# The first tile of x and the first chunk of weights in one transfer, in a 16-batch mixture-of-experts kernel

## The reference

```python
g = einsum('bsd,edf->ebsf', h, Wg)           # E=8, D=128, F=512
u = einsum('bsd,edf->ebsf', h, Wu)
expert_outs = einsum('ebsf,efd->ebsd', silu(g) * u, Wd)
expert_output = einsum('be,ebsd->bsd', gating_probs, expert_outs)
shared = einsum('bsf,fd->bsd', silu(h @ Sg) * (h @ Su), Sd)
x = x + (1.0 - sg) * expert_output + sg * shared
...
x = x + einsum('bij,bjk->bik', T[itok - 1], x)
```

## Time and profile before

| | |
|---|---|
| median of 3 runs | 307.83 us (307.63 to 792.65) |
| the profiled execution's own time | 307.79 us |
| its span in the profile | 306.0 us |
| PE busy / weight loads | 302.3 us (99%) / 250.9 us (82%) |
| DVE, ACT, POOL busy | 214.5, 162.8, 102.2 us |
| instructions | 4476 |

### The profile page before, as it was taken

The page is one execution under the profiler, slowest core; times in us unless marked ns, Lnnn a source line. Parts: engine busy times, 40 slices in busy tenths (PEclk is TensorE's granted clock), DMA queues, the critical chain, the costliest instruction groups (busy, mean ns, idle before and its releaser), DMA issues.

```text
span 306.0 us, 4476 instructions
## 1 busy us (share of the span) xinstructions
PE 302.3 (99%) x1348; PEld 250.9 (82%) x1348; DVE 214.5 (70%) x350; ACT 162.8 (53%) x302; POOL 102.2 (33%) x116
## 2 busy tenths in 40 slices
PE   8999999999999999999999999999999999999996
PEld 8888888888888888888888888888888888888885
DVE  3677667766776676667766776677667666787974
ACT  5755555555555555555555555555555555554562
POOL 3675114431244115511551144311441155700010
PEclk9999999999999999999999999999999999999999
DMA  6700300030002000110003000013000000013242
GB/s 195 261 2 0 104 1 2 0 103 1 0 0 103 0 0 0 28 75 0 0 0 111 26 26 26 26 28 103 0 0 2 0 0 0 2 34 69 43 98 103
DMA packets 13898, 12.00 MB, mean 39 GB/s; under 512 B 6976, under 2 KB 11968, under 8 KB 13888
## 3 DMA queue, kind: packets, MB, share of 16 engines
q1 hardware_dynamic: 13888, 11.87, 12.6%
HBM read 10.04 MB, written 1.84 MB: 39 GB/s over the span
## 4 chain that ended last, share of the span: by engine, by line
PE 98%; DVE 1%; issue 0%
PE o_bank L466 11%; PE o_bank L468 11%; PE o_bank L465 11%; PE u_bank L439 11%; PE u_bank L440 11%; PE u_bank L438 11%; PE g_bank L439 11%; PE g_bank L440 11%; PE g_bank L438 11%; PE o_bank L503 1%; PE o_bank L483 1%; DVE res L377 1%; PE g_bank L483 0%; PE g_bank L510 0%; PE u_bank L510 0%; PE u_bank L478 0%
## 5 line engine op out<-in xcount | busy, mean ns | idle before, releaser
L348 DVE TENSOR_TENSOR u_bank<-u_bank,silu_g 128x512 f32<-128x512 f32 x144 | 100.7, 699 | 82.9 <-PE u_bank L440 81.5
L288 ACT ACTIVATE silu_g<-g_bank 128x512 f32<-128x512 f32 x144 | 86.1, 598 | 133.4 <-PE g_bank L440 132.9
L251 POOL TENSOR_TENSOR acc<-acc,scaled 128x512 f32<-128x512 f32 x32 | 41.4, 1294 | 183.5 <-DVE scaled L362 183.4
L354 DVE TENSOR_TENSOR h_lo<-u_bank,h_hi 128x512 fp32r<-128x512 f32 x144 | 97.9, 680 | 0.1
L294 ACT ACTIVATE h_hi<-u_bank 128x512 fp32r<-128x512 f32 x144 | 85.4, 593 | 0.4 <-DVE u_bank L348 0.4
L465 PE MATMUL o_bank<-h_hi,w_hi 128*128 128x512 f32 x144 | 56.1, 390 | 0.0
L466 PE MATMUL o_bank<-h_hi,w_lo 128*128 128x512 f32 x144 | 56.0, 389 | 0.0
L468 PE MATMUL o_bank<-h_lo,w_hi 128*128 128x512 f32 x144 | 56.0, 389 | 0.0
L438 PE MATMUL u_bank<-x_hi,w_hi 128*128 128x512 f32 x143 | 55.6, 389 | 0.0
L440 PE MATMUL u_bank<-x_hi,w_lo 128*128 128x512 f32 x143 | 55.6, 389 | 0.0
L439 PE MATMUL u_bank<-x_lo,w_hi 128*128 128x512 f32 x143 | 55.6, 389 | 0.0
(11 more groups left out here) (58 smaller groups left out, 143.1 us busy)
## 6 DMA issues: line engine op xcount, KB each, us to landing
w_raw<-in_W_all SPq DMA_DIRECT2D x8, 768.0 KB, 4.4
T_plus<-in_TT SPq DMA_DIRECT2D x16, 64.0 KB, 1.7
turned_y<-yB SPq DMA_DIRECT2D x3, 256.0 KB, 2.3
y<-turned_y SPq DMA_DIRECT2D x12, 64.0 KB, 2.3
out_y<-res SPq DMA_DIRECT2D x3, 256.0 KB, 2.2
acc<-in_xT SPq DMA_DIRECT2D x2, 256.0 KB, 3.9
acc<-in_xT SPq DMA_DIRECT2D x1, 512.0 KB, 5.8
w_raw<-in_W_gu SPq DMA_DIRECT2D x2, 128.0 KB, 3.0
```

What stands on the lines that cost most here:

```text
L251: nc.gpsimd.tensor_tensor(acc[:, t, :], acc[:, t, :], scaled[:, t % 2, :], ALU.add).then_inc(acc_done, 1)
L288: nc.scalar.activation(silu_g[:, k % 2, :], g_bank[k % 2][:, :], ACT.Silu).then_inc(g_read, 1)
L348: nc.vector.tensor_tensor(u_bank[k % HR][:, :], u_bank[k % HR][:, :], silu_g[:, k % 2, :], ALU.mult).then_inc(h_done, 1)
L354: nc.vector.tensor_tensor(h_lo[:, k % HR, :], u_bank[k % HR][:, :], h_hi[:, k % HR, :].bitcast(F32), ALU.subtract).then_inc(split_done, 1)
```

## The change

x tile 0 and chunk 0's gate and up weights are laid side by side in memory on the host (`head`, 128 partitions x 768 fp32, which is 3 KB per partition), and one transfer brings both into a new buffer `head`. `xT` keeps tiles 1 to 3. Who read x tile 0 in `acc` or the weights in `w_raw` reads `head`: DVE's x_hi and x_lo, ACT's w_hi and POOL's w_lo of chunk 0. Later on DVE copies x tile 0 into `acc`, between `make_h(0)` and `make_h(1)`, and POOL waits for that (`x0_kept`) ahead of its loop. On PE the two pairs of matmuls after the first change places: w_lo by x_hi comes ahead of w_hi by x_lo.

```diff
+        head = sb("head", [P, W + 2 * P])
...
-            load_x(0, 1, x_in[0])
-            sp.dma_start(w_raw[:, 0, 0, 0:2, :], W_gu0[:, :, :]).then_inc(wc0_in[0], 16)
+            sp.dma_start(head[:, :], head_in[:, :]).then_inc(head_in_sbuf, 16)
             sp.dma_start(w_raw[:, 0, 1, 0:2, :], W_gu1[:, :, :]).then_inc(wc0_in[1], 16)
...
             pool.wait_ge(w0_rounded, 2)
-            low_part(0, 0, slice(0, 2)).then_inc(w_ready, 1)
+            nc.gpsimd.tensor_tensor(w_lo[:, 0, 0, 0:2, :], head[:, W:W + 2 * P].rearrange("p (m f) -> p m f", m=2),
+                                    w_hi[:, 0, 0, 0:2, :].bitcast(F32), ALU.subtract).then_inc(w_ready, 1)
...
+            pool.wait_ge(x0_kept, 1)
             with pool.Fori(0, E - 2, 2) as e:
...
-            act.wait_ge(wc0_in[0], 16)
+            act.wait_ge(head_in_sbuf, 16)
             for m in range(2):
-                round_w0(0, m)
+                nc.scalar.activation(w_hi[:, 0, 0, m, :], head[:, W + m * P:W + (m + 1) * P], ACT.Copy).then_inc(w0_rounded, 1)
...
-            dve.wait_ge(x_in[0], 16)
-            nc.vector.tensor_copy(x_hi[:, 0, :], acc[:, 0, :]).then_inc(x_rounded, 1)
+            dve.wait_ge(head_in_sbuf, 16)
+            nc.vector.tensor_copy(x_hi[:, 0, :], head[:, 0:W]).then_inc(x_rounded, 1)
             dve.wait_ge(x_rounded, 1)
-            nc.vector.tensor_tensor(x_lo[:, 0, :], acc[:, 0, :], x_hi[:, 0, :].bitcast(F32), ALU.subtract).then_inc(split_done, 1)
+            nc.vector.tensor_tensor(x_lo[:, 0, :], head[:, 0:W], x_hi[:, 0, :].bitcast(F32), ALU.subtract).then_inc(split_done, 1)
...
             make_h(0, 0)
+            nc.vector.tensor_copy(acc[:, 0, :], head[:, 0:W]).then_inc(x0_kept, 1)
             make_h(1, 1)
...
+            pe.wait_ge(w_ready, 1)
+            opening(x_hi, w_lo, False, False)
             pe.wait_ge(split_done, 1)
-            opening(x_lo, w_hi, False, False)
-            pe.wait_ge(w_ready, 1)
-            opening(x_hi, w_lo, False, True)
+            opening(x_lo, w_hi, False, True)
```

More of the change, by code:

```diff
@@ L15, in moe_then_step_kernel @@
     xT: bass.AP,
+    head_in: bass.AP,
     side: bass.AP,
     step: bass.AP,
-    W_gu0: bass.AP,
     W_gu1: bass.AP,
@@ L89, in moe_then_step_kernel @@
         o_bank = [ctx.enter_context(nc.psum_tensor(f"o_bank{i}", [P, W], F32)) for i in range(2)]
+        head_in_sbuf = sem("head_in_sbuf")
+        x0_kept = sem("x0_kept")
         x_in = [sem(f"x_in{i}") for i in range(3)]
@@ L150, in load_x @@
             def load_x(t0, t1, s):
-                sp.dma_start(acc[:, t0:t1, :], xT[t0:t1, :, :].rearrange("t p w -> p t w")).then_inc(s, 16)
-            load_x(0, 1, x_in[0])
-            sp.dma_start(w_raw[:, 0, 0, 0:2, :], W_gu0[:, :, :]).then_inc(wc0_in[0], 16)
+                sp.dma_start(acc[:, t0:t1, :], xT[t0 - 1:t1 - 1, :, :].rearrange("t p w -> p t w")).then_inc(s, 16)
+            sp.dma_start(head[:, :], head_in[:, :]).then_inc(head_in_sbuf, 16)
             sp.dma_start(w_raw[:, 0, 1, 0:2, :], W_gu1[:, :, :]).then_inc(wc0_in[1], 16)
@@ L599 @@
     side = _np.concatenate([_np.asarray(inputs["fside_Bx8_0"]).T.reshape(-1), _np.asarray(inputs["condB_sharedgateprob"])])
+    tiles = x.transpose(2, 0, 1).reshape(D_, 4, -1).transpose(1, 0, 2)
     laid = {
-        "xT": x.transpose(2, 0, 1).reshape(D_, 4, -1).transpose(1, 0, 2),
+        "xT": tiles[1:],
+        "head": _np.concatenate([tiles[0], routed[0, :, 0, 0:2].reshape(P_, -1)], axis=1),
         "side": _np.tile(side[None, :], (P_, 1)),
         "step": _np.asarray(inputs["itok_B_1_98"]),
-        "W_gu0": routed[0, :, 0, 0:2],
         "W_gu1": routed[0, :, 1, 0:2],
```

## The result

The changed kernel takes **309.85 us** (median of 6 runs, 309.11 to 310.20) against 307.79 us before. The medians are 2.06 us or 0.67% apart; the ratio on record, which is not the quotient of the medians, is 1.0055, with a 95% interval of 1.0045 to 1.0065. A few runs last far longer than all others of their kernel (792.65 us here, later 382.45 and 1753.07 us of the kernel before and 622.95 us of e9_hold), and the ratios leave them out. Against a bound of 2% that is no change; it is clear of noise, and it lies above the range of the prediction (307.6 to 309.4). The profiled execution took 310.20 us, which is 2.41 us over the profiled one before.

A forecast was written before the change was run, and what follows sets the result against it. PE was taken to bound the kernel, a shift of its opening carrying whole to the end. 307.79 + 0.50 (swap) + 0.10 (copy) = 308.39, over the median 308.4 us; range 307.6 to 309.4.

The forecast's parts named there:

- What bounds the kernel: Whole kernel: PE is busy for 99% of the span, so a shift of its opening carries whole to the end.
- S = 3.80: Opening: DVE and ACT start together on the merged transfer's data at 3.80 us, between 3.60 and 3.91.
- A little earlier for the weights: Opening: in the merged transfer chunk 0's weights come a little earlier than their 3.91 us, x later than its 3.60.
- Nothing was won at the head: PE's start: its warm-up weight load ends at 4.24 us, so earlier data would win nothing.
- The swap: 0.50 us: PE's unit 0: waiting earlier for POOL's w_lo (0.98 us beside x_lo) makes unit 1 start 0.50 us later, at 6.48.
- the prediction's bound from above: Opening: x_lo holds POOL's w_lo off altogether at first; unit 1 at S + 2.86, a loss of 0.68 to 0.79 us.
- The copy: 0.10 us: Between `make_h(0)` and `make_h(1)`: the gap hides DVE's copy, but slowing POOL's low parts beside it costs PE 0.10 us.
- rival 2: Unit 0's copy: POOL's low part starts first and holds up DVE's copy, 0.50 + 1.05, 309.3 us; chance 0.2.
- The store at the end is untouched: End of the kernel: the change leaves the final store as it was; no cost was counted.
- Rival 3: A case of 12.4 us or more; its description is cut from the prediction's text; chance 0.01.
- The rest: Behind the opening: POOL's wait for `x0_kept` costs nothing and SP's further transfers are issued some 0.44 us earlier.
- Nothing there is on the path: Later transfers and waits: none of them delays PE, which comes to chunk 1's weights only behind unit 0.

The follow-up runs named there:

- e9_hold: e3_both with SP holding back the next expert's 768 KB until expert 0's down weights have landed; median 308.95 us, ratio 1.0024.
- r1_after: The changed kernel, unaltered, timed and traced a second time; median 309.19 us beside 308.09 for the kernel before, ratio 1.0035.
- e4_copy_first: The changed kernel with POOL waiting for DVE's copy of x tile 0 ahead of the low part of the down matrices; 309.39 us, ratio 1.0042.
- e3_both: The changed kernel with PE's old order in unit 0 and the copy moved behind h_lo of unit 2; 308.98 us, ratio 1.0028.
- e14_head_last_in: The changed kernel with `head` given as the last input instead of the second; ratio 1.0038.
- e12_last: The changed kernel with the buffer `head` allocated last, so all other buffers lie where they lay before; 309.97 us, ratio 1.0052.
- e1_pe_order: The changed kernel with PE's old order of unit 0 put back; 309.13 us, ratio 1.0028.
- e2_copy_later: The changed kernel with DVE's copy of x tile 0 moved behind h_lo of unit 2; 309.18 us, ratio 1.0035.
- e10_pad: The kernel before with an unused SBUF buffer of 3 KB per partition added; ratio 0.9995.
- e13_order: The kernel before with `W_gu0` given as the second input instead of the fourth; ratio 1.0011.

## Why the prediction was wrong

It had 307.79 + 0.50 (swap and hold-off) + 0.10 (copy), so 308.4 us, in a range up to 309.4.

1. **What bounds the kernel** held: a shift of the opening is carried whole to the end (+1.93 us at every later sum of POOL).
2. **S = 3.80** held nearly: 3.84 in the profile after, 3.80 to 4.12 in the other traces. "A little earlier for the weights" did not: they are no earlier on the mean (3.93 us over 12 traces, against 3.79 for the second piece over 7). Nothing was won at the head, as forecast.
3. **The swap: 0.50 us.** The mechanism was right, its size came from the wrong one of two readings of one row. I took POOL as slowed in proportion to the overlap (0.98 us); the traces show the other reading, the prediction's bound from above, in which x_lo holds POOL off altogether at first (1.15 us). The hold-off is gone 0.53 to 0.55 us behind the start of x_lo, ahead of the end of its row of 0.69 us. That reading gave unit 1 at S + 2.86; r1_after shows S + 2.80. The measured loss there is 6.76 - 5.98 = 0.78 us: of the 0.28 us that the forecast lacked, 0.12 is this reading (2.80 for 2.68) and 0.16 the later S (3.96 for 3.80).
4. **The copy: 0.10 us.** This is the step that failed, and rival 2, at 0.2, was the case in all five traces with the copy in its place: POOL first, the copy held up. It was priced at 1.05 us and measured 0.8 to 0.95 in the traces. I named the race and its margin of under 0.1 us rightly, and then let one row decide it (a DVE operation that starts up to 0.1 us ahead of the end of its forerunner). In the trace DVE does start early, at 8.32, 0.61 us after the start of a `make_h(0)` of 0.70 us, but POOL starts at 8.28. e4_copy_first shows the same copy at 0.41 us when the order is turned.
5. **"The store at the end is untouched."** Untouched in the code, and 0.44 to 0.50 us longer in every kernel with an `xT` of 768 KB. No term and no rival had it. With the copy it takes the time out of the range: 308.4 + 0.85 (copy, 0.95 for 0.10) + 0.28 (swap, 0.78 for 0.50) + 0.48 = 310.0 us, against 309.85. That the sum comes so near the median is in part luck: its terms are from traces of executions with the copy held up.
6. **Rival 3**, with its chance of 0.01, stood for PE running at a lower clock behind its new gap for 12.4 us or more. No run shows such a stretch or what it costs: the granted clock reads 1.00 from 3.5 to 12 us in both traces of the changed kernel, and r1_after has loads of 0.19 us behind a gap of 0.57 us. What did come is that slow loads end by chance between 4.0 and 6.9 us, which the earlier trace rows hinted at (0.29 against 0.19 us). I had no term for it; it cost 0.47 us in the first trace of the changed kernel (S + 3.27 for S + 2.80) and up to 0.9 us elsewhere.
7. **The rest** held in the traces of the changed kernel. "Nothing there is on the path" was too strong for its variants: the weights of chunks 2 and 3 landed late in some, and in e3_both PE waited 0.52 us for POOL's w_lo of them.

Open: the second timing of the changed kernel, at 309.19 us, would have fallen into the range. Four of the five runs of r1_after lie at 309.12 to 309.25 us, while the profiled one, with the copy held up, took 309.86; e14_head_last_in splits in the same way, and the first timing (two of six runs at 309.1, four at 309.8 to 310.2) and e12_last (two of six at 309.2 to 309.4) in part. That fits executions in which the copy comes first, some 0.7 us better, and would explain why e1_pe_order and e2_copy_later gain so little in their medians: without the copy the terms give 0.78 + 0.48 = 1.26 us over the kernel before, against 1.10 in r1_after, and e2_copy_later, where nothing holds the copy up, has its median in the same place, 309.18. Against it stands e4_copy_first: there the copy comes first in every run, and all five lie at 309.29 to 309.40, above this group, as its trace is only 0.42 us better than those with the copy held up (36.15 against 36.57). So it is argued only, and what the faster executions do is not shown; no trace of one was had. In seven of the kernels the profiled execution is also the slowest of all runs (changed, r1_after, e1_pe_order, e2_copy_later, e3_both, e10_pad and e14_head_last_in), so another cause that lengthens that one alone is not excluded.

## What to carry to other kernels

Merging two transfers makes two consumers start at once; ask what these consumers do to each other (here DVE's subtraction from SBUF against POOL's) before counting the issue that is saved, and price two such operations side by side as nearly serial (POOL's w_lo took 1.15 us beside x_lo and 0.73 without it, the copy 1.53 us behind POOL's start and 0.41 ahead of it). Not every pair is such a one: `make_h`, which reads u from PE's bank and only one operand from SBUF, takes 0.70 us beside POOL's low parts (7.74 us before), which is its mean over all 144 (699 ns). Where two operations on DVE and POOL are released by the same event within 0.1 us, take the bad order as the price, or fix the order. Changing how inputs are split can move time at the far end of the kernel, here 0.44 to 0.50 us: compare the landing times of transfers that the change doesn't touch.

## What was not expected of the hardware

- The size of one input tensor in HBM (768 KB for 1 MB, with the same bytes read) changes the landing of stores to another tensor from 2.2 or 2.3 to 2.5 or 2.6 us. The order of the inputs (2.2 us in e13_order, 2.6 in e14_head_last_in) and 3 KB in SBUF (2.2 in e10_pad, 2.6 in e12_last) change nothing.
- PE's first weight loads behind the warm-up take 0.27 to 0.34 us in 13 of the 19 traces, and turn to 0.19 us at a point that varies by execution; the first of 0.20 us or less starts between 4.02 and 6.86 us, with and without idle of PE ahead of it. The granted clock reads 1.00 over all of that stretch, so this row doesn't show it; the durations of the loads do.
- The two first matmuls behind PE's wait for h_lo of unit 0 start 0.34 us apart instead of 0.23 (11.10 and 11.44 in the changed kernel, 10.75 and 11.09 in r1_after), those behind the wait for POOL's w_lo 0.33 (5.75 and 6.08 in r1_after), and 0.60 where the loads are slow (5.63 and 6.23 in the changed kernel).
